# Attention's slots on TensorE taken in pairs: two transposes, then two products

## What is computed

```
xn = layernorm(x, g_in)
q = (xn @ Wq) split into 16 heads of 64, scaled;  k, v = split(xn @ Wkv)
k, v = the null key and value ahead of k, v
sim = q k^T + bias,  causal mask, key mask
out = softmax(sim) v,  heads side by side,  @ Wo,  layernorm
```

## Time and profile before

| | us |
|---|---|
| median of 3 runs | 1331.17 |
| lowest to highest | 1330.85 to 1332.63 |
| profiled execution | 1329.25 |
| its span, first to last instruction | 1327.5 |

### The profile page before, as it was taken

One profiled execution on the slowest core, in us unless ns is written; L12 is line 12 of the kernel. 1 busy time (PEld: TensorE's weight loads), 2 busy tenths in 40 slices (PEclk: granted clock), 3 DMA queues, 4 the chain that ended last, 5 costly groups with the idle time before them and its releaser, 6 DMA issues. The chain is left out here.

```text
span 1327.5 us, 23485 instructions
## 1 busy us (share of the span) xinstructions
PE 1002.6 (76%) x6466; PEld 874.2 (66%) x6467; DVE 802.7 (60%) x2155; ACT 628.2 (47%) x1483; POOL 740.6 (56%) x864
## 2 busy tenths in 40 slices
PE   4859999999999999999998034767725454089986
PEld 3638888888888888878887034667723343078885
DVE  6137767677676767766675574866636756634442
ACT  1126665676666666666665022333312121466553
POOL 1138778888788887878785014505520452624343
PEclk9759999999999999999999555878868676589998
DMA  6154545556555555555550601313338011234443
GB/s 166 53 173 124 167 148 159 168 152 180 147 157 178 153 174 153 156 163 157 149 151 11 217 6 62 102 43 124 119 129 338 32 67 38 96 66 76 65 77 38
DMA packets 111587, 163.70 MB, mean 123 GB/s; under 512 B 16023, under 2 KB 85143, under 8 KB 110456
## 3 DMA queue, kind: packets, MB, share of 16 engines
q1 hardware_dynamic: 100406, 143.21, 36.0%
q0 software_dynamic: 10560, 19.18, 6.2%
q10 hardware_dynamic: 514, 0.04, 0.0%
HBM read 111.68 MB, written 25.53 MB: 103 GB/s over the span
## 5 line engine op out<-in xcount | busy, mean ns | idle before, releaser
L1707 POOL TENSOR_SCALAR probs<-probs,inv_sum 128x1024 f32<-128x1024 f32 (+7 forms) x256 | 439.3, 1729 | 125.5 <-DVE inv_sum L1842 125.3
L1757 ACT ACTIVATE probs<-probs,neg_max 128x1025 f32<-128x1025 f32 (+7 forms) x256 | 200.9, 785 | 115.4 <-POOL probs L1696 107.8
L1810 DVE CUSTOM_DVE_ANT_0 probs<-s_ps,bias_set,neg_null 128x512 f32<-128x512 f32 (+3 forms) x256 | 166.0, 649 | 112.2 <-PE s_ps L1871 110.2
L1739 ACT ACTIVATE pT_hi<-t_ps 128x512 fp32r<-128x512 f32 (+1 forms) x320 | 177.2, 554 | 70.0 <-PE t_ps L1902 69.6
L1832 DVE TENSOR_TENSOR pT_lo<-t_ps,pT_hi 128x512 fp32r<-128x512 f32 (+1 forms) x320 | 201.9, 632 | 11.7 <-ACT pT_hi L1739 11.5
L1922 PE MATMUL o_ps<-pT_hi,values 128*128 128x256 f32 x576 | 174.1, 322 | 23.7 <-DVE pT_lo L1832 22.8
L1902 PE MATMUL t_ps<-ident,probs 128*128 128x128 f32 x1152 | 180.3, 275 | 12.3 <-POOL probs L1707 6.5
L1870 PE MATMUL s_ps<-k_hi,q_hilo 128*128 128x512 f32 (+3 forms) x384 | 161.3, 420 | 8.8 <-DMA q_one<-q_hi 7.5
L1902 PEld LDWEIGHTS t_ps<-ident,probs 128*128 128x128 f32 x1152 | 140.7, 141 | 39.4 <-issue 7.9
L1923 PE MATMUL o_ps<-pT_lo,values 128*128 128x256 f32 x576 | 150.6, 281 | 0.0
L1871 PE MATMUL s_ps<-k_lo,q_one 128*128 128x512 f32 (+3 forms) x384 | 136.0, 354 | 0.0
(11 more groups left out here) (301 smaller groups left out, 2075.6 us busy)
## 6 DMA issues: line engine op xcount, KB each, us to landing
bias_set<-bias_dram SPq DMA_DIRECT2D x16, 1024.0 KB, 5.1
bias_set<-bias_dram SPq DMA_DIRECT2D x16, 896.0 KB, 5.0
bias_set<-bias_dram SPq DMA_DIRECT2D x16, 768.0 KB, 4.8
bias_set<-bias_dram SPq DMA_DIRECT2D x16, 640.0 KB, 4.4
q_hilo<-q_hi SPq DMA_DIRECT2D x128, 64.0 KB, 2.0
q_hilo<-q_lo SPq DMA_DIRECT2D x128, 64.0 KB, 2.0
q_one<-q_hi SPq DMA_DIRECT2D x128, 64.0 KB, 2.0
bias_set<-bias_dram SPq DMA_DIRECT2D x16, 512.0 KB, 5.2
```

Source lines behind the costliest of these rows:

```text
L1707: last = pool.tensor_scalar(keys, keys, inv_sum[:, x.set, unit, h:h + 1], None, ALU.mult)
L1739: act.activation(pT_hi[n % 3][:, 0:count, :], t_ps[TURNS["slot", n] % 3][:, 0:2 * P * count], ACT.Copy).then_inc(hi_out, 1)
L1757: act.activation(p, p, ACT.Exp, scale=-1.0, bias=neg_max[:, x.set, row.unit, h:h + 1], accum_out=row_sum[:, x.set, row.unit, h:h + 1]).the ...
L1810: dve.tensor_tensor_reduce(probs_row(x, row, h)[:, 1 + P * first:1 + P * (first + count)], s_ps[e % 2][:, 0:P * count], bias_row(x, row, h ...
```

## The change

Only TensorE's list changes. Slots are taken in pairs n, n + 1 with n even: the first item of `SCORES_AT[n]`, `turn(n + 2)` and `turn(n + 3)` one behind the other, the other items of slot n, `weigh(n)`, all items of slot n + 1, the projection that slot n - 1 ended, `weigh(n + 1)`, and the projection that slot n ended. The instructions, the buffers and the waits of each are the same. The lists of the other engines stay. As a step has five slots, the pairs of one step begin at its slots 0, 2 and 4, and those of the next at its slots 1 and 3.

```diff
@@ -1944,17 +1944,24 @@
                     fill(item)
                 for n in range(2):
                     turn(n)
-                for n in range(NS + 3):
-                    if n < NS:
-                        for item in SCORES_AT[n][:1]:
-                            fill(item)
-                        turn(n + 2)
-                        for item in SCORES_AT[n][1:]:
-                            fill(item)
-                        weigh(n)
+                for n in range(0, NS, 2):
+                    for item in SCORES_AT[n][:1]:
+                        fill(item)
+                    turn(n + 2)
+                    turn(n + 3)
+                    for item in SCORES_AT[n][1:]:
+                        fill(item)
+                    weigh(n)
+                    for item in SCORES_AT[n + 1]:
+                        fill(item)
                     ended = ends_at(n - 1)
                     if ended:
                         project(*ended)
+                    weigh(n + 1)
+                    ended = ends_at(n)
+                    if ended:
+                        project(*ended)
+                project(*ends_at(NS - 1))
 
 
 def program(nc, x, bias, cond, mask, g_in, nab, Wq, Wkv, Wo, out, routed_rows, parts, **aps):
```

## The result

| | before | after |
|---|---|---|
| median of the runs, us | 1331.01 | 1359.1 |
| lowest to highest | 1326.03 to 1332.63 | 1350.19 to 1365.13 |
| profiled execution, us | 1329.25 | 1365.13 |
| its span | 1327.5 | 1363.4 |

The ratio is 1.0193, with a 95% interval from 1.0152 to 1.0234: slower, clear of noise; whether by more than 2% these runs leave open. The forecast was 1356 us.

What follows compares the result with a forecast made beforehand. TensorE's stream was taken to bound the attention stage, each step holding a latency behind the query projection. The terms 13.2 + 10.5 + 6 - 2.6 - 2 = +25.1 us on the 1331.17 us median gave 1356 us, range 1338 to 1370.

Steps and rivals of the forecast that it cites:

- What bounds, and where the hole is: Attention stage: TensorE's stream sets the time, with a 0.84 us hole before slot 3's value products, from the query's chain.
- Part 1: Pairs opening at slot 2: four transposes move from behind the query projection to ahead of it, 30 x 0.44 = +13.2 us.
- Part 2: Even steps: those moved transposes newly wait for slot 2's low half on VectorE, 30 x 0.35 = +10.5 us, 3 to 18.
- Part 3: Ends of seven inner rounds: the null weights' transpose waits for one low half more, +6 us, from 2 to 9.
- Part 4: Give-backs: a low-half wait in the second tile pair mostly gone, -2.6 us, and 160 fewer runs of transposes, -2 us.
- The alternation: Sign: distances between query projections alternate, about 9.8 and 10.6 us where both were 9.84.
- N's wait: Sign: at round ends the null weights' transpose is idle for 0.7 us or more.
- The hole before W3: Sign: in even steps a hole of about 1.2 us before slot 3's products with the values, directly behind its scores.
- The wait on L1902: Sign: TensorE's transposes wait for low halves some 25 to 35 us in sum where there were 5.9.
- Switching is what costs: Rival: each removed run of transposes saves 0.08 to 0.17 us, so the kernel gets faster, 1320 us; chance 0.07.
- the hole is only moved: Rival: the odd steps' hole and VectorE's slack absorb what even steps lose, 1331 to 1333 us; chance 0.05.
- the waits feed each other: Rival: late transposes make the query, other engines' loop and the null weights late, 1371 to 1379 us; chance 0.15.

Runs made afterwards that it cites:

- e1: Changed kernel, but in pairs opening at slot 2 the second slot's transposes stand behind the query projection again; stage 636.9 us, ratio to before 1.0103.
- e2: Kernel before, with only the next step's slot 0 transposes moved ahead of the query projection in every second step; stage 650.5 us, ratio 1.0193.
- e7: Changed kernel with round ends taken singly and, in pairs opening at slot 2, the second transposes behind the query projection; stage 628.6 us, ratio to before 1.0004.
- e3: Kernel before, with each run of four transposes cut in two by the slot's first score chunk; stage 647.6 us, ratio 1.0188.
- e10: Changed kernel without its two costly places, and with VectorE taking the next slot's low half ahead of the query's; stage 604.0 us, ratio to before 0.9835.
- The control of the switches' test: Kernel before, with each slot's transposes whole but ahead of its first score chunk; stage 672.3 us, ratio 1.0346.
- e8: Kernel before, with the query projection ahead of the transposes in slot 2; stage 618.5 us, ratio 0.9944.

## Why the prediction was right, and where it wasn't

1. **What bounds, and where the hole is.** Right. Taking the low half off the query's chain removed the hole and 24 us.
2. **Part 1, T5 leaves the cover (+13.2).** Right in mechanism and size. T5 to Q is 0.46 us, and the latency from Q to W3 stayed (155.81 - 153.16 = 2.65 us). With T5's wait taken off (item 3), the place costs 15.5 - 2.7 = 12.8 us by e1, and 22.4 - 9.6 = 12.8 us by e2. By the figure of the Trainium skill ("TensorE: Matmul & The Clock Gate", Part 4: PE-mode transpose), about 275 ns for one, the four would take 1.1 us, an estimate; the runs decide for the spacing of the rows.
3. **Part 2, T5's new wait (+10.5).** The mechanism was right, the size about four times too large. Parts 1 and 2 together cost 15.5 us, not 23.7. In the first tile pair T4 and T5 take 1.02 us in the timeline of after where 0.82 is their work. By the starts of T4 and T5 the wait is 0.16, 0.06, 0.19 and 0.00 us in the four tile pairs, 2.7 us in all 30 steps, where I took 0.35 a step. The step that failed: I took the time at which low half 2 is ready from the rows of before, where it starts 1.62 us behind low half 1, and added that S0b comes late. S0b did come late: low half 1 starts 3.01 us after S0a in the timeline of after (147.53 to 150.54), 2.77 us before. But low half 2 starts only 1.33 us behind it, as VectorE's timeline shows (low half 1, scores, low half 2):

```profile
150.54 0.69 DVE L1832 TENSOR_TENSOR pT_lo<-t_ps,pT_hi 128x512 fp32r<-128x512 f32 x1
...
151.22 0.73 DVE L1810 CUSTOM_DVE_ANT_0 probs<-s_ps,bias_set,neg_null 128x512 f32<-128x512 f32 x1
...
151.87 0.68 DVE L1832 TENSOR_TENSOR pT_lo<-t_ps,pT_hi 128x512 fp32r<-128x512 f32 x1
```

   The scores start at 151.22, at once behind the reciprocal, where before VectorE idled 0.19 us for TensorE's chunk S1. In the pair the projection P4 (0.83 us) stands behind S1 and no longer ahead of it; T3 (0.44 us) now stands ahead, so S1's second half starts 2.68 us after S0a, and 3.13 before. On TensorE (the second half of S1, then P4):

```profile
150.21 0.40 PE L1871 MATMUL s_ps<-k_lo,q_one 128*128 128x512 f32 x1
150.45 1.03 PE L1932 MATMUL y_ps<-wo,oT 128*128 128x256 f32 x4
```

   My sum had this new order in T5's need and not in its supply. e2 bears this out: there P4 stays ahead of S1, T5 waits 0.28, 0.38, 0.50 and 0.04 us in the four tile pairs, 9.6 us in all, near the 10.5, and the two parts cost 22.4 us, near the 23.7. That it is P4's place, among all that differs between the two, is read from the timelines; no run moves P4 alone.
4. **Part 3, the round's end (+6).** Right in mechanism, too small: 9.3 us, just above the range of 2 to 9. The null weights' transpose waits 1.04 us, a little more than the 0.7 to 1.0 that I gave, and T5 behind it another 1.03, as it did before:

```profile
181.82 0.82 PE L1902 MATMUL t_ps<-ident,probs 128*128 128x128 f32 x6
183.68 0.38 PE L1911 MATMUL t_ps<-ident,null_w 128*16 128x128 f32 x2 [1.04 <-DVE pT_lo L1832]
...
184.84 1.05 PE L1880 MATMUL s_ps<-xnT,wq_all 128*128 128x128 f32 x8
...
187.57 1.17 PE L1902 MATMUL t_ps<-ident,probs 128*128 128x128 f32 x8 [1.03 <-DVE pT_lo L1832]
```

5. **Part 4, the give-backs (-4.6).** Wrong. Pairs that add no wait gave back nothing: e7 is 0.5 us above before. The 0.16 us of the second tile pair was not banked, and a switch costs what rows 4 said, nothing that can be told; the 2 us that I booked for it anyway had no row behind them.
6. **The sum.** +24.3 in the stage against +25.1 forecast, and +28.1 in the medians. That the sum was this close was in part luck, as its terms missed in opposite directions: 8 too much in part 2, 3 too little in part 3, 5 given back that didn't come. Of the 28.1 us in the medians the change's own part is the 24.3; the rest is of the kind of the head and the tail.
7. **Signs named ahead.** The alternation came (9.7 and 10.8), and N's wait. The hole before W3 of 1.2 us in even steps came as 0.94 of idle. The wait on L1902 came as 16.7 us, not 25 to 35, which is part 2's error again. The rest of the kernel was not quite unchanged (3.4 us and the head).
8. **Rivals.** "Switching is what costs" fell with e7 and the first tile pair of e3; "the hole is only moved" with e1 and e2; "the waits feed each other" isn't seen: the pairs' costs by place add up (24.8 for 24.3).

## What to carry to other kernels

Where an engine issues the head of a latency chain and waits at its end, the work that it does in between is free. Reordering it ahead of the head cost nearly its full length here (12.8 us of 13.2), though no instruction was added. Moving more work in gained less (9.6 us of 18 expected), as something else soon held the step. Look at such a hole as a stock of cover, and better still take the waiting item off the chain: a swap of two items on VectorE was worth as much (24 us) as the change lost. The same work can cover more than one chain. When a need is moved earlier, work out anew when its supply comes in the new order; rows of the old order price it wrong.

## What the runs showed of the hardware

**TensorE's clock ahead of the stage.** The first transpose of the stage starts at 90.5 us (e10) to 104.3 us (e7), in kernels whose code up to there is the same. In the windows view the granted clock is the number right ahead of the DMA share (the last but two). Before:

```profile
33.00:45.00 12.00, 12.00 (x67) 7.99 (x66) 0.68 (x1) 3.13 (x5) 0.00 (x0) 0.86 0.01 1
45.00:55.00 10.00, 10.00 (x57) 7.02 (x56) 1.87 (x3) 1.94 (x4) 0.00 (x0) 0.83 0.00 0
```

After:

```profile
33.00:45.00 12.00, 12.00 (x51) 8.36 (x50) 0.68 (x1) 1.77 (x3) 0.00 (x0) 0.66 0.01 1
45.00:55.00 10.00, 10.00 (x36) 6.05 (x34) 0.00 (x0) 1.37 (x2) 0.00 (x0) 0.50 0.00 0
```

The control of the switches' test:

```profile
33.00:45.00 12.00, 12.00 (x76) 7.85 (x74) 0.68 (x1) 3.12 (x5) 0.00 (x0) 1.00 0.01 1
45.00:55.00 10.00, 10.00 (x69) 8.85 (x67) 1.97 (x3) 1.94 (x4) 0.00 (x0) 0.88 0.00 0
```

TensorE is busy in all of both stretches. The clock is 0.86 and 0.83 in the first, 0.66 and 0.50 in the second, 1.00 and 0.88 in the third; the stage starts at 95.1, 103.3 and 92.1 us. So TensorE drops from 2.4 to 1.2 GHz at another time in each execution, though it is never idle there. The mean clock from 25 us to the stage's start goes the same way: 0.79 in e10, 0.73 in the control, 0.69 before, 0.66 after. By these means (an estimate) TensorE was at half speed for 27 us in e10 and 53 in after, which makes 13 us, and the starts are 12.8 apart; between before and after it makes 5 of the 8.2 us. The start of the stage moves by up to 1% of the kernel's time in this way. What makes the clock drop, no run here shows. I had booked the head as constant.

**Switches.** Going between transposes in float32 and products in the rounded format costs nothing to be seen: in the timeline of e8 above, the second transpose starts 0.11 us after 462.95, and the second product behind it at 463.29, 0.23 us later, which is one spacing of each kind (0.11 and 0.12). A run of eight projection matmuls behind a score chunk was 0.1 us longer than behind transposes.
